# Order of the first loads, who clears the accumulator, 22 row tiles and five places for the stray checks, in a graph layer on one core

## The reference

```python
h = jnp.maximum(_layernorm(x, axis=-1), 0.0)
msg = jax.nn.relu(h[src] + edge_attr)
agg = jax.ops.segment_sum(msg, dst, num_segments=x.shape[0])
h = h + agg
h = jax.nn.relu(h @ W1 + b1)
x = x + (h @ W2 + b2)
```

## Time and profile before

| what | value |
|---|---|
| time, median of 3 executions | 1404.91 us (1401.84 to 1407.89) |
| profiled execution, own time | 1406.43 us |
| its span, first to last instruction | 1404.6 us |
| mean granted TensorE clock | 0.991 |
| busy: PE, DVE, ACT, POOL | 1369.4, 1216.5, 1063.3, 1057.5 us |
| one-row DMAs | 2560 |
| gathers from `h_table` | 1091 |
| DMA loads of edges | 62 x 832 KB |

### The profile page before, as it was taken

The page is one execution under the profiler, slowest core; times in us unless marked ns, Lnnn a source line. Parts: engine busy times, 40 slices in busy tenths (PEclk is TensorE's granted clock), DMA queues, the critical chain, the costliest instruction groups (busy, mean ns, idle before and its releaser), DMA issues.

```text
span 1404.6 us, 26588 instructions
## 1 busy us (share of the span) xinstructions
PE 1369.4 (97%) x7788; PEld 708.6 (50%) x7788; DVE 1216.5 (87%) x1869; ACT 1063.3 (76%) x1165; POOL 1057.5 (75%) x1114
## 2 busy tenths in 40 slices
PE   7897999999999999999999999999999999999997
PEld 4443555555555555555555555555555555555554
DVE  8698988888888888888888888888888989878887
ACT  6775877787777877777777777887787777877772
POOL 7777777777777777777777777777777777777775
PEclk8999999999999999999999999999999999999999
DMA  7223233233232332333323233233232323323231
GB/s 247 65 58 83 73 91 86 70 95 85 69 90 66 94 85 69 90 74 86 85 68 95 68 88 85 69 95 86 70 85 69 95 68 88 85 69 94 62 86 29
DMA packets 70785, 116.54 MB, mean 83 GB/s; under 512 B 34522, under 2 KB 35950, under 8 KB 70638
## 3 DMA queue, kind: packets, MB, share of 16 engines
q1 hardware_dynamic: 34302, 76.39, 17.3%
q0 software_dynamic: 35328, 36.25, 13.1%
q10 hardware_dynamic: 1008, 2.19, 0.4%
HBM read 111.39 MB, written 3.34 MB: 82 GB/s over the span
## 4 chain that ended last, share of the span: by engine, by line
PE 82%; DVE 6%; POOL 5%; ACT 2%; issue 2%; DMA 1%; DVEq 0%; SPq 0%; POOLq 0%; ACTq 0%
PE ps_cand L1305 80%; POOL gath L397 5%; PE ps L426 1%; DVE parts L1027 1%; ACT keyhot L738 1%; DVE gath L979 1%; DVE picked L972 1%; DMA gath<-h_table,idx_all 1%; ACT keyhot L745 1%; DMA src_k<-src_keys 1%; PE ps L460 1%; DVE ends L1037 1%; DVE ps_edge L1020 1%; DVE table_lo L899 0%; PE ps L450 0%
## 5 line engine op out<-in xcount | busy, mean ns | idle before, releaser
L397 POOL DMA_INDIRECT gath<-h_table,idx_all x1091 | 1040.9, 954 | 334.4 <-issue 316.5
L1305 PE MATMUL ps_cand<-table_hi,keyhot 128*128 128x448 f16 x3388 | 1197.3, 353 | 18.0 <-DVE picked L972 13.7
L1305 PE MATMUL ps_cand<-table_lo,keyhot 128*128 128x448 f16 x3388 | 1196.2, 353 | 0.0
L738 ACT ACTIVATE keyhot<-key_pair,key_bias 128x512 f16<-128x512 f16 (+1 forms) x854 | 532.6, 705 | 115.1 <-PE ps_cand L1305 113.9
L1305 PEld LDWEIGHTS ps_cand<-table_hi,keyhot 128*128 128x128 f16 x3388 | 331.8, 98 | 333.0 <-DVE picked L972 9.7
L1305 PEld LDWEIGHTS ps_cand<-table_lo,keyhot 128*128 128x128 f16 x3388 | 332.0, 98 | 301.3 <-issue 2.0
L745 ACT ACTIVATE keyhot<-keyhot,hot_bias 128x3584 f16<-128x3584 f16 (+1 forms) x122 | 397.4, 3258 | 3.9
L972 DVE TENSOR_TENSOR picked<-ps_cand,cand_mask 128x448 f32<-128x448 f32 x488 | 301.3, 617 | 81.8 <-PE ps_cand L1305 81.4
L979 DVE TENSOR_REDUCE gath<-picked 128x64 f32<-128x448 f32 x488 | 298.6, 612 | 4.2
L1027 DVE SCALAR_TENSOR_TENSOR parts<-ps_edge,side 128x832 f32<-128x832 f32 x242 | 235.3, 1014 | 0.0
L1037 DVE TENSOR_REDUCE ends<-parts 128x128 f32<-128x1664 f32 x122 | 228.7, 1875 | 0.0
(11 more groups left out here) (112 smaller groups left out, 189.2 us busy)
## 6 DMA issues: line engine op xcount, KB each, us to landing
edge_pair<-edges_t SPq DMA_DIRECT2D x62, 832.0 KB
gath<-h_table SPq DMA_DIRECT2D x2560, 0.2 KB
gath<-h_table,idx_all POOLq DMA_INDIRECT x1091, 2.4
key_pair<-key_table SPq DMA_DIRECT2D x61, 256.0 KB
h_table<-h_a SPq DMA_DIRECT2D x7, 224.0 KB, 2.7
part_x<-x_t SPq DMA_DIRECT2D x29, 48.0 KB
out<-part_out SPq DMA_DIRECT2D x29, 48.0 KB
x_c<-x_cols ACTq DMA_DIRECT2D x4, 256.0 KB, 4.7
```

The source lines that it names most:

```text
L397: nc.gpsimd.indirect_dma_start(out=rows[:, r, :], out_offset=None, in_=h_table, in_offset=bass.IndirectOffsetOnAxis(ap=idx[:, r:r + 1], ax ...
L738: last = nc.scalar.activation(keyhot[u % 2][:, a, 0:n], key[u][:, P * PE_MAX - n:], ACT.Abs, bias=key_bias[:, a:a + 1])
L1305: last = nc.tensor.matmul(bank[:, 0:D * CAND], keyhot[u % 2][:, a, i * P:(i + 1) * P], half[:, a, :, :].rearrange("p d b -> p (d b)"), sta ...
```

## The change

There are four edits.

1. *Loads.* Targets (`dst_i`, 806 KB), bases (`base_i`) and candidates (`src_c`, 248 KB) were issued by ScalarE right after its part of `x`. Now SyncE issues them, after it has waited for the keys (`src_k`, 256 KB) to land, and the first two edge loads (832 KB each) follow behind them.
2. *Clearing.* GpSimd's clearing is gone. VectorE clears 4500 columns instead of 3000, ScalarE the other 1844, with a copy of scale 0, ahead of its second `deviation`.
3. *Row tiles.* `ROWS_AT` is (30, 18), which makes 22 row tiles of 2816 rows. `ROW_CHUNKS` and `PE_SPARED` follow: the spared chunks were (5,1), (12,2), (19,3), (27,0) and are (4,3), (11,2), (18,1), (24,2).
4. *Checks.* `outside_edges` is split into `extreme_places`, `least_rooms` and the rest; the five functions run one a turn, after the second slot of turns 2 to 6.

```diff
--- before.py
+++ after.py
@@ -76,7 +76,7 @@
 CAND = GROUP
 
 
-ROWS_AT = (28, 16)
+ROWS_AT = (30, 18)
 ROWS_A_LOAD = 16
 ROW_TILES = (TURNS - 1) * PAIRS * sum(ROWS_AT) // P
 
@@ -98,7 +98,7 @@
 PAIRED = -(-GROUP // 2)
 WAKES = 8
 KEYS_AFTER = 3
-DVE_ZEROS = 3000
+DVE_ZEROS = 4500
 CAND_BANKS = 4
 F16 = mybir.dt.float16
 BF16 = mybir.dt.bfloat16
@@ -487,6 +487,10 @@
             for g in range(3, N_GROUPS, 2):
                 sp.dma_start(x_c[:, x_piece(g)], x_cols[:, x_piece(g)]).then_inc(x_loaded[g], 16)
             sp.dma_start(src_k[:, :], src_keys).then_inc(keys_loaded, 16)
+            sp.wait_ge(keys_loaded, 16)
+            sp.dma_start(src_c[:, :, :], src_cands).then_inc(meta_loaded, 16)
+            sp.dma_start(dst_i[:, :, :], dst_t).then_inc(meta_loaded, 16)
+            sp.dma_start(base_i[:, :], base_t.partition_broadcast(P)).then_inc(meta_loaded, 16)
             for h in range(PAIRS):
                 sp.dma_start(edge_pair[h][:, :, :, :], edges_t[:, h * PAIR:(h + 1) * PAIR, :, :]
                              ).then_inc(edge_loaded[h], 16)
@@ -618,9 +622,6 @@
 
 
 
-            pool.wait_ge(part_ends_made, 2)
-            nc.gpsimd.memset(agg[D:2 * D, DVE_ZEROS:], 0.0).then_inc(odd_half_zeroed, 1)
-
             def gather_first():
 
                 for r in range(TILES_PER_CHUNK):
@@ -671,10 +672,6 @@
         def _(act):
             for g in range(0, N_GROUPS, 2):
                 act.dma_start(x_c[:, x_piece(g)], x_cols[:, x_piece(g)]).then_inc(x_loaded[g], 16)
-            act.dma_start(dst_i[:, :, :], dst_t).then_inc(meta_loaded, 16)
-            act.dma_start(base_i[:, :], base_t.partition_broadcast(P)).then_inc(meta_loaded, 16)
-            act.dma_start(src_c[:, :, :], src_cands).then_inc(meta_loaded, 16)
-
             act.wait_ge(consts_made, 1)
             nc.scalar.activation(root_seen[:, :], eps_col[:, :], ACT.Sqrt)
 
@@ -694,6 +691,9 @@
             deviation(range(FIRST_HALF))
             for g in range(FIRST_HALF + 1, N_GROUPS):
                 square(g)
+            act.wait_ge(ident_made, 1)
+            nc.scalar.activation(agg[D:2 * D, DVE_ZEROS:], iota_f[D:2 * D, 0:1].to_broadcast([D, AGG_COLS - DVE_ZEROS]),
+                                 ACT.Copy, scale=0.0).then_inc(odd_half_zeroed, 1)
             deviation(range(FIRST_HALF, N_GROUPS))
 
             def spread_keys():
@@ -937,14 +937,18 @@
             def least_covered():
                 then(nc.vector.tensor_reduce(side_min[:, :], stray[:, :, :], mybir.AxisListType.XY, ALU.min))
 
-            def outside_edges():
+            def extreme_places():
                 then(nc.vector.tensor_reduce(place_max[:, :], place[:, :, :], mybir.AxisListType.XY, ALU.max))
                 then(nc.vector.tensor_reduce(place_min[:, :], place[:, :, :], mybir.AxisListType.XY, ALU.min))
+
+            def least_rooms():
                 then(nc.vector.tensor_copy(base_f[:, :], base_i[:, :]))
                 dve.wait_ge(part_ends_made, 2)
                 then(nc.vector.tensor_tensor(room[:, :], base_i[:, :], part_ends_i[:, :], ALU.subtract))
                 then(nc.vector.tensor_reduce(least_room[:, :], room[:, :], AX_X, ALU.min))
                 then(nc.vector.tensor_reduce(last_base[:, :], base_f[:, LAST_CHUNK:], AX_X, ALU.min))
+
+            def outside_edges():
                 then(nc.vector.tensor_scalar(low[:, :], place_min[:, :], 0.0, None, ALU.is_lt))
                 then(nc.vector.scalar_tensor_tensor(out=apart[:, :], in0=side_min[:, :], scalar=1.0,
                                                     in1=low[:, :], op0=ALU.is_lt, op1=ALU.max))
@@ -1151,15 +1155,16 @@
                     sides(FAR_CHUNKS, u)
                 if u == ENDS:
                     window_places(FAR_CHUNKS)
-            covered_edges()
-            least_covered()
-            outside_edges()
+            checks = {FIRST_PART_TURN: covered_edges, FIRST_PART_TURN + 1: least_covered, FIRST_PART_TURN + 2: extreme_places,
+                      FIRST_PART_TURN + 3: least_rooms, FIRST_PART_TURN + 4: outside_edges}
             dve.wait_ge(weights_loaded, 16 * WEIGHT_LOADS)
             base_before = window_base(TURNS - 2, SLOTS - 1)
             bases = [window_base(TURNS - 1, u) for u in range(SLOTS)]
             for t in range(FIRST_PART_TURN, TURNS):
                 for u in range(SLOTS):
                     chunk(t, u, between=t if u == SLOTS - 1 else None)
+                    if u == 1 and t in checks:
+                        checks[t]()
             t, u = TURNS - 1, SLOTS - 1
             accumulate(t - 1, u, base_before, 1)
             accumulate(t, 0, bases[0])
```

## The result

The changed kernel takes 1518.87 us (median of five executions, 1518.69 to 1522.35), against 1404.91 for the kernel before. The ratio is 1.0816, with a 95% interval of 1.0799 to 1.0833: 8.2% slower, far outside the predicted range of 1396.6 to 1405.4. The profiled execution took 1522.35, its span is 1520.6, so the profile shows the whole loss.

The account below looks back on a forecast made before the run. GpSimd's unbroken column of 1091 gathers was taken to bound the kernel; 2.5 us from two gathers fewer plus 2.0 from the start made 4.5, so 1400.4 us from the median of 1404.91, range 1396.6 to 1405.4.

Parts of the forecast that it names:

- 22 row tiles: Loop: two GpSimd gathers fewer, 2.5 us less; SyncE's added 135 to 159 us fit within its 183.3 us of waits.
- Rival D: SyncE's queue in the loop becomes the bound, at 1 us more per turn than reckoned: 1413 us; chance 0.06.
- lead of 17 us: Loop: SyncE may fall about 17 us behind before late keys make anyone wait.
- The clearing: Start: without GpSimd's clearing, `ident` gives VectorE 2.7 us back; VectorE's clearing grows 1.3 us, ScalarE's costs 0.
- Keys first: Start: VectorE takes the keys 2.4 us earlier, at 9.6, and GpSimd's early gathers move up, 2.0 us less.
- rival A: The start gives nothing, as stores end late or a gather is held: 1402.4 us; chance 0.15.
- The checks, 0 on the end: Turns 2 to 6: spreading the checks gives TensorE 6.6 us back, but it doesn't end last: gain 0.
- The product over all sides: A 1.83 us check instruction, still run in turn 2, delays a GpSimd gather: 0.9 us gained to 0.3 lost, taken as 0.

Follow-up runs that it names:

- e6: The changed kernel with (30, 18) kept and the table of places laid out so every load starts at a multiple of 16: 1406.33 us, ratio 0.9986.
- e2: The changed kernel with ROWS_AT put back to (28, 16), all other edits kept: 1408.35 us, ratio 1.0008 to the kernel before.
- e3: The changed kernel with ROWS_AT = (32, 16) instead of (30, 18): 1403.44 us, ratio 0.9989 to the kernel before.
- e8: As e3, without SyncE's wait for the keys: 1403.32 us, ratio 0.9988 to the kernel before.
- e12: As e10, with the checks spread over five turns as in the change: 1402.67 us, ratio 0.9987 to the kernel before.
- e10: The kernel before with ROWS_AT = (32, 16) and nothing else of the change: 1402.89 us, ratio 0.9975.
- e9: As e3, with all five check functions in one run, as before the change: 1406.80 us, ratio 1.0011 to the kernel before.
- e7: The kernel before with 20 extra table loads after its last turn, from columns 64 to 67: 16 places took 1.16 us from 64, 3.50 from the others.
- e4: The changed kernel with ROWS_AT = (28, 20), so every load starts at a multiple of four: 1406.95 us, ratio 0.9992 to the kernel before.
- e5: The kernel before with ROWS_AT = (30, 14), its second share starting two columns off a multiple of four: 1406.85 us, ratio 1.0002.

## Why the prediction was wrong, point by point

**The step that failed** is the price of a table load in "22 row tiles": "a load costs 10.54 - 28 x 0.32 = 1.6, or 1.1 by the shorter group of 10.05". The shorter group was read rightly: its load of 12 places took 1.02, with some 0.14 around it, and one of 16 takes 1.18. The longer group holds the same load of 12 (1.02), so its 1.6 was no load's price. But every load in that trace begins at a multiple of four, since 28, 44 and 16 are such multiples. The new shares begin elsewhere, at 48k + 30. The table loads' sum rose not by 48 loads x 1.1 to 1.6 = 53 to 77 us but by 187, of which 51 x (3.55 - 1.20) = 120 is the second share's load of 16 places, read one by one. With the rows' 256 x 0.32 = 82, SyncE got 269 us more, not 135 to 159. It had 183.3, and 17 remain; the 103 left over make most of the loss of 114, and the other 11 were not traced.

The arithmetic around that price was sound. e6 has the change's counts with aligned loads: 68 us of loads and 82 of rows, 150, inside the predicted 135 to 159, and a wait of 20.8 (and 4.1 more at the loads) where 24 to 48 were predicted.

**Rival D** named the mechanism and the chain of waits, which the trace of after shows, and a lead of 17 us, which fits roughly. Its price was "1 us more than now reckoned per turn"; the turn came out at 48.3, 4.6 above the 43.7 of the kernels that SyncE doesn't bound. Its sign, waits of GpSimd for candidates of over 1 us, is there too (up to 6.8). Its sum was also off by its own numbers: of 2.8 us of wait per half turn it has 2.3 to 2.7 used, and the 6 to 29 us that this leaves over 58 half turns would have been used up before the lead. It got 0.06 because the one thing that could make it large, a load dearer than any in the trace, was treated as a scatter of a few per cent. The prediction asked what the trace shows of a load; it should have asked in which form (count, first column) and whether the change keeps it.

**22 row tiles, 2.5 us less**: right where SyncE keeps up. In e2 the last gather starts at 1395.98, in e3 at 1393.46.

**The clearing**: right. `ident` took 0.29 us in place of 2.91, VectorE's clearing 3.81, ScalarE's 1.74 (at most 2.3 was said), and its second deviation no longer waited.

**Keys first**: right on VectorE (keys taken at 9.54, predicted 9.3 to 10.7; `h_a` done at 17.45, predicted 17.6), wrong on the stores. They were to land at 22.1 and landed at 25.8, as the DMA engines ran at 190 to 249 GB/s up to 16 us where 377 was assumed (how much of the 3.7 us that makes was not taken apart), and the third gather started at 28.57, not 26.7. This is rival A, down to the sign that was named for it (28 or later); e2 bears it out: a ratio of 1.0008 where 2 us of gain were predicted for the start. The prediction cited a rule for A (the Trainium skill, DMA: Bandwidth & Descriptors, "Queues, rings and completion order"), that a queue's descriptors are consumed in order. e8 agrees as far as it goes: with the loads issued earlier on the same queue the stores landed 2.9 us earlier than in e3. What no part of the prediction had was the 4 us that TensorE loses by the late keys of the loop.

**The checks, 0 on the end**: right against the kernel before, as far as e12 against e10 shows, and for the reason given. TensorE's hole of 7.3 us at 115 is gone from the changed kernel (its longest wait for picks is 2.8). But with gathers removed and a late TensorE they were worth 3.4 us (e9): the two engines lie within 2 us of each other (e3's wait of 3.47 is 1.8 above the least), and "not what ends last" holds only for the start that was assumed. The product over all sides did what was said: it runs at 138.27 in the changed kernel and holds one gather for 2.24 us instead of 0.95 (timeline of after):

```profile
138.27 1.83 DVE L935 TENSOR_TENSOR x_sq<-side 128x1612 f32<-128x1612 f32 x1
...
138.68 2.24 POOL L397 DMA_INDIRECT gath<-h_table,idx_all  x1 [0.30 <-issue]
```

## What to carry to other kernels

When a change alters where an instruction's operand begins or how many elements it has, its price from the old trace is only a price for the old form: list the forms (count, first column) before and after, and measure each new one alone before multiplying it. An engine with much idle time can carry added work at no cost until the idle time is used up, and from there each microsecond per turn costs the number of turns; so the margin that remains is worth as much attention as the sum. A load put off behind a wait moves all that stands behind it on its queue: read that queue to the loop's first use, on every engine.

## What the runs showed of the hardware

- **Table loads.** From a column that is a multiple of four (16 bytes), 16 places take about 1.2 us (1.16 in e7); from columns one, two or three further, 3.5. Fourteen places take 1.46, more than sixteen. Two take 0.73, more than four (0.56).
- **TensorE's clock after a wait.** Behind the wait of 7.3 us at the checks the granted clock is 0.50 (1.2 GHz) in a stretch of e9, and 1.00 in the same stretch of e3, which has no such wait.
- **GpSimd's step has two values.** From the 101st to the 1089th gather, e3 goes from 156.09 to 1393.46, 1.2524 us a step, and e10 from 157.49 to 1392.11, 1.2496. Before, e2, e4, e6 and e8 have 1.2521 to 1.2526; e5, e9, e10 and e12 have 1.2495 to 1.2502. e9 and e3 ran on the same chip in the same set, so it isn't the chip alone. Over 1089 gathers this is 3 us, about the spread of a kernel's executions. Its cause is open, and gains of 2 us can't be read from single profiles. e3, the 101st gather and the last:

```profile
156.09 0.96 POOL L397 DMA_INDIRECT gath<-h_table,idx_all  x1 [0.30 <-issue]
1393.46 0.95 POOL L397 DMA_INDIRECT gath<-h_table,idx_all  x1 [0.30 <-issue]
```

e10, the same two gathers:

```profile
157.49 0.95 POOL L397 DMA_INDIRECT gath<-h_table,idx_all  x1 [0.30 <-PE ps_cand L1305]
1392.11 0.94 POOL L397 DMA_INDIRECT gath<-h_table,idx_all  x1 [0.30 <-issue]
```
